# Where the keys' norm is multiplied in: the values' copies on ScalarE instead of the cubed keys on VectorE

## The reference, cut to what matters

```python
q, k = (relu(q) + 1e-6) / scale, (relu(k) + 1e-6) / scale
k_norm = norm(k)                       # over all 256 channels of a token
k = k ** 3
k = k / norm(k) * k_norm               # the same for q
z = 1.0 / (einsum('bic,bc->bi', q, k.sum(axis=1)) + 1e-6)
kv_state = einsum('bjc,bjd->bcd', k, v)             # 8 heads of 32
out = einsum('bic,bcd->bid', q, kv_state) * z[..., None]
out = out + depthwise_conv_5x5(v)                   # then the projection
```

## Time and profile before

| | |
|---|---|
| median of 3 runs | 3855.68 us (3854.17 to 3865.21) |
| the profiled execution, its own time | 3868.91 us |
| its span | 3867.1 us |
| PE busy (matmuls) | 3532.3 us, 91% |
| PEld busy (weight loads) | 2857.3 us, 74% |
| DVE busy | 2762.7 us, 71% |
| ACT busy | 2651.2 us, 69% |
| POOL busy | 1596.4 us, 41% |
| mean granted TensorE clock | 0.978 |
| chain that ended last | PE 57%, DVE 12%, issue 11%, ACT 9%, DMA 6% |

### The profile page before, as it was taken

One profiled execution on the slowest core, in us unless ns is written; L12 is line 12 of the kernel. 1 busy time (PEld: TensorE's weight loads), 2 busy tenths in 40 slices (PEclk: granted clock), 3 DMA queues, 4 the chain that ended last, 5 costly groups with the idle time before them and its releaser, 6 DMA issues.

```text
span 3867.1 us, 94623 instructions
## 1 busy us (share of the span) xinstructions
PE 3532.3 (91%) x27988; PEld 2857.3 (74%) x27988; DVE 2762.7 (71%) x6715; ACT 2651.2 (69%) x7096; POOL 1596.4 (41%) x1557
## 2 busy tenths in 40 slices
PE   1679999999999999999999999999999999999897
PEld 1248787777877778787777878777787777878786
DVE  7776776767677676777767677676767767575747
ACT  2347676766777677677766767676676767677675
POOL 4551443615345261544526254361535436150402
PEclk9889999999999999999999999999999999999999
DMA  6652634436353453635446263443626344360302
GB/s 217 210 182 73 187 118 139 141 116 177 101 171 111 138 170 91 192 112 151 128 122 190 78 189 112 141 144 114 194 79 184 111 137 135 92 184 13 110 12 77
DMA packets 560058, 516.59 MB, mean 134 GB/s; under 512 B 97601, under 2 KB 491969, under 8 KB 559553
## 3 DMA queue, kind: packets, MB, share of 16 engines
q1 hardware_dynamic: 555200, 508.99, 43.6%
q10 hardware_dynamic: 4352, 1.57, 0.2%
HBM read 351.06 MB, written 134.22 MB: 125 GB/s over the span
## 4 chain that ended last, share of the span: by engine, by line
PE 57%; DVE 12%; issue 11%; ACT 9%; DMA 6%; POOL 2%; SPq 2%; DVEq 1%; ACTq 0%; POOLq 0%
PE F L1541 11%; PE SM L1524 9%; PE VAB L1541 7%; PE F L1580 6%; PE T L1552 5%; PE VAB L1580 5%; DMA PL<-xp 5%; PE PP L1632 4%; PE VAB L1610 3%; ACT K L1308 3%; PE F L1543 2%; PE T L1601 2%; DVE F L996 1%; PE T L1620 1%; SPq L352 1%
## 5 line engine op out<-in xcount | busy, mean ns | idle before, releaser
L1541 PE MATMUL F<-WQ,XHL 128*128 128x256 f16 x6144 | 817.3, 274 | 27.4 <-ACT V L1345 19.1
L636 POOL TENSOR_TENSOR SL<-PL,SL 128x1122 f16<-128x1122 f32 x112 | 259.8, 2320 | 1067.2 <-DVE SL L970 1067.2
L661 POOL TENSOR_TENSOR XR<-XR,V 128x512 f32<-128x512 f32 x256 | 325.9, 1273 | 898.0 <-DVE XR L1057 898.0
L1541 PEld LDWEIGHTS F<-WQ,XHL 128*128 128x128 f16 (+1 forms) x6144 | 601.0, 98 | 103.7 <-issue 33.7
L1314 ACT ACTIVATE K<-K,SCAL 128x256 f32<-128x256 f32 x1024 | 512.6, 505 | 192.2 <-DVE K L1002 191.8
L1308 ACT ACTIVATE K<-F,SCAL 128x256 f32<-128x256 f32 x1024 | 474.8, 469 | 242.9 <-DVE F L996 240.0
L1524 PE MATMUL SM<-SL,BD 128*128 128x512 f16 x2688 | 634.9, 385 | 0.0
L1002 DVE TENSOR_TENSOR K<-K,F 128x512 f32<-128x512 f32 x512 | 350.4, 684 | 273.6 <-ACT K L1308 138.8
L1524 PEld LDWEIGHTS SM<-SL,BD 128*128 128x128 f16 x2688 | 260.9, 97 | 284.2
L996 DVE TENSOR_TENSOR F<-F,FL 128x512 f32<-128x512 f32 x512 | 353.6, 691 | 157.3 <-PE F L1543 152.9
L1632 PE MATMUL PP<-XR,WP 128*128 128x256 f16 x3072 | 385.5, 276 | 48.9 <-DVE XR L1075 48.9
(11 more groups left out here) (202 smaller groups left out, 6858.4 us busy)
## 6 DMA issues: line engine op xcount, KB each, us to landing
XR<-xr SPq DMA_DIRECT2D x132, 512.0 KB, 5.3
U<-x SPq DMA_DIRECT2D x256, 256.0 KB, 3.5
XR<-x SPq DMA_DIRECT2D x256, 256.0 KB, 4.2
out<-XR SPq DMA_DIRECT2D x256, 256.0 KB, 3.7
PL<-xp SPq DMA_DIRECT2D x112, 561.0 KB, 3.9
RX<-xr SPq DMA_DIRECT2D x118, 512.0 KB, 3.8
x<-RX SPq DMA_DIRECT2D x448, 128.0 KB, 2.7
BD<-RX SPq DMA_DIRECT2D x240, 96.0 KB, 2.2
```

Of the source, the lines that this page charges most:

```text
L661: g_.tensor_tensor(o, o, fm, ALU.add).then_inc(o_rdy, 2)
L1541: t_.matmul(o, XHL[:, xa, h, at], WQ[:, wa, h, c0:c0 + C], start=(k == 0), stop=False)
```

## The change

VectorE's `scale_k` is gone, and the cubed keys stay unscaled in `K3`. ScalarE's two copies of the values into `VT` now have the keys' norm of their token (`NORM`) as scale instead of the constant `inv_a`. As that norm is known a step later, the copies are made a step later (`scaled_v` of the step before, between `norms` and the high half), and they wait for the norm (`f_root`), for the buffer (`cube_used`) and for `low_v` (`v_lo`). TensorE's values wait for these copies as well, since they read `VA`. VectorE writes the norms into column 129 of `VT` in each step (`sum_column`, four elements for each partition), in the place that `scale_k` had; GpSimd's column of ones and TensorE's wait for it are gone. The constant `inv_a` is applied when the state is copied out of `T` (a `tensor_scalar` in place of a `tensor_copy`, eight times in a batch). `low_v` no longer waits for the copies into `VT`. After the last step `low_v` is moved ahead of `ratio`.

```diff
-            def scale_k(n, p):
-                dve.wait_ge(f_root, n + 1)
-                ks = K3[:, p, :].rearrange("p (t n) -> p t n", t=2)
-                v.tensor_tensor(ks, ks, NORM[:, 2 * p:2 * p + 2].unsqueeze(2).broadcast_to([P, 2, C]), ALU.mult
-                                ).then_inc(k_scaled, 1)
+            def sum_column(b, u, p):
+
+                m = b * PAIRS + 2 * u + p
+                dve.wait_ge(f_root, b * 2 * PAIRS + 2 * u + p + 1)
+                dve.wait_ge(cube_used, b * 2 * PAIRS + 2 * u + p + 1)
+                v.tensor_copy(VT[:, p, :, :, P:P + 1].rearrange("p t h o -> p t (h o)"),
+                              NORM[:, 2 * p:2 * p + 2].unsqueeze(2).broadcast_to([P, 2, HALVES])).then_inc(sum_col, 1)
...
                 dve.wait_ge(v_hi, m + 1)
-                dve.wait_ge(v_true, m + 1)
...
                 cube(n, p)
-                scale_k(n - 1, 1 - p)
+                sum_column(b, u - 1 + p, 1 - p)
...
-                        v.tensor_copy(KVS[r, h, o_v + q:o_v + P:HPH], T[h][r, q:P:HPH]).then_inc(state_rdy, 1)
+                        v.tensor_scalar(KVS[r, h, o_v + q:o_v + P:HPH], T[h][r, q:P:HPH], inv_a[r, :], None, ALU.mult
+                                        ).then_inc(state_rdy, 1)
...
-                if keys_end and p == 0:
-                    scale_k(n - 2, 0)
...
                 low_v(b, 0, 0)
+                sum_column(b, 0, 0)
...
+                low_v(b, NU - 1, 1)
                 ratio(n, 1, S2, S6)
-                scale_k(n, 1)
-                low_v(b, NU - 1, 1)
+                sum_column(b, NU - 1, 1)
...
             ratio(0, 0, S2, S6)
-            scale_k(0, 0)
             cube(1, 1)
...
-            def copy_v(b, u, p):
+            def high_v(b, u, p):
...
+            def scaled_v(b, u, p):
                 act.wait_ge(cube_used, b * 2 * PAIRS + 2 * u + p + 1)
+                act.wait_ge(f_root, b * 2 * PAIRS + 2 * u + p + 1)
+
+                act.wait_ge(v_lo, b * PAIRS + 2 * u + p + 1 + VLO_CR)
                 for t in range(2):
                     ins = a.activation(
                         VT[:, p, t, :, 0:P].rearrange("p h (c f) -> p h c f", c=HD),
                         VA[p][:, :].rearrange("p (c t h f) -> p t h c f", c=HD, t=2, h=HALVES)[:, t],
-                        ACT.Copy, scale=inv_a)
+                        ACT.Copy, scale=NORM[:, 2 * p + t:2 * p + t + 1])
...
                 norms(n - 1, 1 - p, inv_a2)
-                copy_v(b, u, p)
+                scaled_v(b, u - 1 + p, 1 - p)
+                high_v(b, u, p)
...
-                for p in range(2):
-                    copy_v(b, 0, p)
+                high_v(b, 0, 0)
+                scaled_v(b, 0, 0)
+                high_v(b, 0, 1)
...
                 norms(b * 2 * PAIRS + PAIRS - 1, 1, inv_a2)
+                scaled_v(b, NU - 1, 1)
...
-                pe.wait_ge(k_scaled, m + 1)
-                pe.wait_ge(v_true, m + 1)
+                pe.wait_ge(sum_col, m + 1)
+                pe.wait_ge(v_true, m + 1 + VT_CR)
...
                 pe.wait_ge(v_lo, b * PAIRS + 2 * u + p + 1)
+                pe.wait_ge(v_true, b * PAIRS + 2 * u + p + 1)
                 project(b, u, p, VA, 2 * C)
...
-                pe.wait_ge(ones_rdy, b + 1)
-                carry(pe)
```

More of the change, by code:

```diff
@@ L218, in conv_then_focused_attention @@
         f_cube, f_six, f_ratio, f_root = sem("f_cube"), sem("f_six"), sem("f_ratio"), sem("f_root")
-        k_scaled, cube_used = sem("k_scaled"), sem("cube_used")
+        cube_used = sem("cube_used")
         v_full, v_hi, v_true, v_lo = sem("v_full"), sem("v_hi"), sem("v_true"), sem("v_lo")
-        ones_rdy = sem("ones_rdy")
+        sum_col = sem("sum_col")
         state_full, state_rdy = sem("state_full"), sem("state_rdy")
@@ L230, in conv_then_focused_attention @@
         VLO_CR, FM_CR, O_CR, OL_CR, Y_CR = 2, 4, 2, 2, 2
-        AT_CR, OUT_CR, QT_CR, Z_CR = 1, 1, 1, 4
+        AT_CR, OUT_CR, QT_CR, Z_CR, VT_CR = 1, 1, 1, 4, 2
         N_W, N_C = 5, 8
@@ L661, in add_depthwise @@
                 g_.tensor_tensor(o, o, fm, ALU.add).then_inc(o_rdy, 2)
-            def ones():
-                g_.memset(VT[:, :, :, :, P:P + 1], 1.0).then_inc(ones_rdy, 1)
             def batch(b, ahead):
@@ L682, in batch @@
                 if s1:
-                    pool.wait_ge(attn_full, (b + 1) * NT + AT_CR)
-                    carry(pool)
-                    ones()
                     for u in (NU + 1, NU + 2):
@@ L729, in _ @@
                          (ol_rdy, OL_CR), (cube_used, USED_CR), (z_rdy, Z_CR),
-                         (y_rdy, Y_CR), (attn_full, AT_CR), (qt_rdy, QT_CR)):
+                         (y_rdy, Y_CR), (v_true, VT_CR), (attn_full, AT_CR), (qt_rdy, QT_CR)):
                 dve.sem_inc(s, n)
```

## The result

The changed kernel takes 3902.99 us (median; 3890.22 to 3908.28), beside 3856.42 us (3854.17 to 3865.21) for the kernel before on the same chip. The ratio, taken over all runs and not from the two medians, is 1.0099 with a 95% interval of 1.0082 to 1.0116: slower by 1%, some 38 us, where "no change" was forecast with 3858 us. (The medians lie 46.6 us apart, the spans of the two profiled executions 39.4; the five runs of each spread over 11 and 18 us, so the loss is known as about 40 us.) Even the range, which ended at 3883, doesn't hold it.

A forecast was written before the change was run, and what follows sets the result against it. TensorE was taken as the bound. -1.8 + 4.8 - 1.7 - 2.4 + 3.4 = +2.3 us turned the profiled 3868.9 into 3871.2, or 3858 us for the median, called no change; range for 8 in 10: 3844 to 3883.

The forecast's parts named there:

- Undisturbed steps: Key steps without GpSimd's rotation: TensorE sets their 3.95 us, so removing VectorE's 0.69 us of scaling gains nothing.
- Disturbed steps: Key steps during GpSimd's rotation: 4.4 us gained from ended waits, 2.6 lost to late norms, net -1.8 us.
- The rival: Key steps in rotation lock to GpSimd's instruction pair, some six steps a batch 0.45 us longer: 3883 us, chance 0.17.
- The end of the stage: Last key step, 16 times: later norm and longer copies add 0.3 us each, +4.8 us; bounds 0.1 and 0.5 each.
- The start of batch 0: Once, in the first batch: a cube is no longer held up behind a wait for a norm, -1.7 us.
- The rest: Before a batch's first projection: TensorE's wait for the ones goes, 0.2 us in 12 batches, -2.4 us; other edits nothing.
- The clock: Behind the key stage's end: two more ends fall to TensorE's slow clock, +3.4 us, ends -17 and +10.
- the rival of the lock: Key steps in rotation take GpSimd's period because VectorE's tiny instructions are held: 3883 us, chance 0.17.
- the end's upper bound: Last key step of each batch: at most 0.5 us longer, where 0.3 was taken.
- the clock's upper bound: Behind the key stage's end: all sixteen ends at TensorE's slow clock, +10 us where +3.4 was taken.

The follow-up runs named there:

- a_norot: The changed kernel without GpSimd's rotation of kernels in the key stages (output not the reference's): 3873.02 us, 1.0040 of the kernel before.
- a_col: The changed kernel with the sum column alone written by ScalarE instead of VectorE: 3883.28 us, 1.0054 of the kernel before.
- a_ratio: The changed kernel with the key steps' reciprocal in PSUM, so the ratio's multiply reads one SBUF input: 3869.26 us, 1.0030 of the kernel before.
- a_rf: The changed kernel with the ratio's reciprocal in PSUM and useless products (8 and 12) in both gaps of the stage's end: 3852.82 us, 0.9978 of the kernel before.
- b_rf: The kernel before with the ratio's reciprocal in PSUM and useless products (10 and 6) in both end gaps: 3849.24 us, 0.9973 of the unmodified one.
- a_fill: The changed kernel with 8 and 12 useless TensorE products in the two gaps of the stage's end: 3872.88 us, 1.0026 of the kernel before.
- b_fill: The kernel before with 10 and 6 useless TensorE products in the two gaps of the stage's end: 3857.87 us, 0.9987 of the unmodified one.
- a_f2: The changed kernel with 12 useless TensorE products in the second gap of the stage's end alone: 3874.18 us, 1.0041 of the kernel before.

## Why the prediction was wrong

**Undisturbed steps.** Right. They stay at 3.95 us (ScalarE's idle time before the squares is 0.18 to 0.20 us, where near 0.3 was said), and the key stages of the last two batches are 60.8 where 60.6 was said.

**Disturbed steps** (-1.8 us): the step that failed, and the larger error. It put down 2.6 us for late norms; without the rotation the changed kernel's steps are 23.2 us shorter (a_norot), and against the kernel before they cost 18.0 net. The working took 0.05 us for ScalarE to see its own norm; it is 0.17 in every step, so the slack of 0.75 us was 0.12 smaller. More weight lies on the claim that "a first delay leaves part of the next inside ScalarE's reserve": it was priced from a single hold, though the text had a second one, in the column copy, and let that one cost nothing. a_col shows the ratio's hold alone at 0.5 us a batch, already more than the 0.2 taken. Two holds in one step cost about 1.7 us a batch (23 us in the 14 batches that rotate, between the changed kernel and a_ratio). The rival had mechanism and period right; its count of steps was too high (six of 4.40 us; there are about four, with a mean of 4.38), and its threshold, a self-wait of 0.25 us, too late, since the lock came at 0.17 with both holds. It was given a chance of 0.17. The size of the self-wait alone wasn't varied; how much it contributes stays open.

**The end of the stage** (+4.8 us): mis-sized. At full clock it is +8.5 to +8.7 us (a_rf against b_rf, a_fill against b_fill), 0.54 in a batch, just over the bound of 0.5. From norm to outer products it takes 1031.41 - 1030.06 = 1.35 us for 1.07, so +0.28 where 0.15 to 0.2 was said; 0.12 of it is the self-wait (0.17 for 0.05). The norm is 0.26 later (1030.06 - 1026.30 = 3.76 us behind step 13's products, for 3.50), where 0.1 to 0.15 was said.

**The start of batch 0** (-1.7 us): right, a little more. TensorE's wait of 6.12 us in the earlier trace rows is 3.96 now, 2.2 less.

**The rest** (-2.4 us): right. From L1669 to the first keys it is 0.71 to 0.75 us in the loop, for 1.00 in the earlier trace rows: 12 x 0.24 = 2.9 us. It didn't reach the time: TensorE's "issue" wait ahead of L1669 is 19.8 us for 10.6, and in the starts of the batches TensorE is at 1.2 GHz for 34 us, where it was 19. Why is open, as said at a_fill.

**The clock** (+3.4 us, ends -17 and +10): the mechanism was right, the size wrong. The text counted slow ends and held their length at 3.4 us. The count rose to 14, near the twelve named, but eight of them last twice as long, and most of the time at 1.2 GHz fell into the depthwise stage. It doubled, from 37.5 to 75.1 us in ends and depthwise stages. By the two filled kernels it is worth 28 us in the changed kernel and 13 in the one before, +15 where +3.4 was said and +10 was the bound. That is somewhat over a third of the time at 1.2 GHz; the text had taken half (1.7 of 3.4 us).

In sum, 18.0 for the steps and 21.9 for ends and depthwise stages make 39.9 us; the spans differ by 39.4. Of the 21.9, 15.1 are the clock and 6.8 stand at full clock (8.7 in the ends, less 1.9 in the depthwise stages). The rest nearly cancels: the start-up is 2.1 us longer, the starts of the batches 3.4, the query stages 5.8 shorter.

The range was too narrow for one more reason: the rival of the lock, the end's upper bound and the clock's upper bound were treated as separate cases. They came together. The self-wait is part of the second; whether the first needs it isn't shown.

## What to carry to other kernels

When a change hangs a buffer's release behind a tiny instruction, ask of that instruction how many SBUF inputs it reads and what runs on GpSimd beside it. Here a reciprocal written to PSUM in place of SBUF was worth 0.7% of the kernel's time. Price two holds in one step together and not one by one: here one was absorbed for the most part, and two locked the step to the other engine's period. And where a change makes the end of a stage sparser for TensorE, add to its price what the lower clock behind it costs; a few products of no use are a cheap probe for that.

## What the runs showed of the hardware

- ScalarE waits 0.17 us from the end of a two-column norm until its next instruction, which reads the result, starts (0.46 us from start to start, where an independent one follows after 0.19).
- A VectorE copy of four columns from SBUF to SBUF took 154 ns at least and 1312 at most beside GpSimd (1425 in a_ratio); a multiply of two columns 160 and 1387 with both inputs in SBUF, 156 and 157 with one in PSUM (512 and 240 of them).
- A copy of 32 x 32 out of PSUM took 0.21 us, the same with a multiply by a value for each partition 0.27.
- Twelve products of no use (a_f2) in a sparse stretch kept TensorE at 2.4 GHz behind it in 16 ends of 16; ends and depthwise stages together went from 651.1 to 622.5 us, 1.8 us for each.
- Three kernels with the same two gaps (2.60 and 1.97 us from start to start) had 10, 5 and 6 slow ends of 16, in one execution each.
